# Attention and expert layer, one Trainium2 core: the context of four heads is split on GpSimd and turned by a DMA transpose

## The chip, the cores and the metric

The kernel runs on one core of one Trainium2 chip. The metric is the device time of one execution in microseconds (us), taken as the median of several runs.

## What is computed

The input x has 8 batches of 512 tokens with 256 features. The result is x plus two branches:

```python
xn = layernorm(x)
q, k, v = split(xn @ qkv_w.T)            # 16 heads of 64
q, k = rope(q), rope(k)
attn = softmax(q @ k.T / 8 - p * log1p(a * |i - j|))
out1 = concat_heads(attn @ v) @ out_w.T
out2 = top-1 mixture of 16 experts (relu(x @ w1) @ w2), capacity 256 rows each, scaled by the gate
result = x + out1 + out2
```

Everything is float32 in the reference. The kernel keeps that accuracy on TensorE by writing a float32 operand as the sum of two fp16 parts, a high and a low one, and by summing three products: high by high, high by low and low by high.

## The kernel before, in words

Three stages follow one another: `prepare` (norms, weights, routing), `experts`, and `attention`. The change lies wholly in `attention`, which fills the time from about 326 us to the end.

**Batches, groups and slots.** `attention` goes through 8 batches (the first and the last are written out, the six between are a hardware loop). A batch has 4 groups j of four heads, and a group has 8 slots k; slot l = 8j + k handles two tiles of 128 queries of one head. Each engine runs its own `slot(b, l)`, in an order that is written out by hand and held together by counting semaphores:

- TensorE: the scores of the slot (L1282, L1283), one "fill" of the PSUM bank `ps_x`, the transposes of the probabilities of slot l-1 into `ps_t` (L1294, 8 of them), and the products with the values of slot l-2 into `ps_o` (L1319, 24 of them).
- VectorE: the row minimum of the negated scores (L1187, twice), the reading of a fill, the low fp16 part of the turned probabilities (`pair_lo`, L1144), and after every fourth slot `read_context` (L1160, L1162), which divides `ps_o` by the sums of the softmax and writes the context `ctxt`.
- ScalarE: the copy of a fill, the high fp16 part of the turned probabilities (`pair_hi`, L1066), and two exponentials (L1085).

**Fills.** In slots k = 0 to 5 of a group TensorE projects the queries, keys and values of a group two ahead (`qk` L1249, `v` L1259). In slots k = 6 and 7 it multiplies the context of the group that ended one before by the output weights (`y`, L1269), and VectorE adds this to `yacc` (L1138).

**The context's way before the change.** The context of a group is complete when VectorE has done `read_context` in slot k = 2 of the next group. In slot k = 3 TensorE turns it (`context_transposes`, L1303, eight 128x128 transposes) into one of the two `ps_t` tiles that the probabilities use in turn. ScalarE writes its high part (`ctx_hi`, L1071) and VectorE its low part (`ctx_lo`, L1150) to `ot`, and the `y` fills of slots 6 and 7 read `ot`. The first group has no predecessor, and the last one's context is turned behind the last slot; so there are 32 such steps.

**GpSimd** rotates the queries and keys of the group two ahead: `turn` for w = 0 and 1 (four products L1003 into `prod`, a difference L1006 and a sum L1007 into `rot`), then the low parts (L1014) after ScalarE's high parts (L1060, in slots 5 and 7). In the groups j = 0 and 1 it also issues two gathers each (L1023).

**SyncE's queue** (SP) runs `move` once for each group that is projected: when GpSimd has written the second low part it issues 16 DMAs of 64 KB (L963), waits until they have landed, and issues two DMAs of 256 KB (`kswap`, L967). It also loads the next batch's activations (`xcur`, L970, in group j = 1) and the routes of a batch (L975, L976, at its start). ScalarE's queue stores `yacc` in slot 9 and loads it in slot 11 (L1094, L1097), 512 KB each.

Of the kernel before, what the change touches and what calls it, by code (L numbers as in the profile page):

```python
# [830 lines left out]
def attention(nc, sem, x, out, xt_dram, xcur, x_loaded, expert_dram, source_dram, gate_dram, ident, wt, wot, cos, sin,  # L831
# [8 lines left out]
    with ExitStack() as ctx:  # L840
# [4 lines left out]
        prod = sb("prod", [P, 4, S])  # L845
# [12 lines left out]
        ctxt = sb("ctxt", [P, TPB, HG * D])  # L858
        ot = [sb(f"ot_{n}", [P, 2, S], F16) for n in ("hi", "lo")]
# [44 lines left out]
        def pair_item(l):  # L904

            return 9 * (l // 8) + l % 8 + (l % 8 > 3)

        def items(b, n):

            if isinstance(b, int) and b == 0:  # L910
                return n + 1 - (n >= 0) - (n >= 4)
            return 36 * b + n + 1 - 2
# [83 lines left out]
        def _(pool):  # L996
            def turn(F, w, n):
# [4 lines left out]
                for i, (half, table) in enumerate(((0, cos), (1, sin), (0, sin), (1, cos))):  # L1002
                    nc.gpsimd.tensor_tensor(prod[:, i, :], proj[:, w, half, :], table[:], ALU.mult).then_inc(turned_parts, 1)  # L1003
                pool.wait_ge(turned_parts, done + 4)
                wait(pool, parts_lo, 2 * F - 1 + w)
                nc.gpsimd.tensor_tensor(rot[:, w, 0, :], prod[:, 0, :], prod[:, 1, :], ALU.subtract).then_inc(turned_parts, 1)  # L1006
                nc.gpsimd.tensor_tensor(rot[:, w, 1, :], prod[:, 2, :], prod[:, 3, :], ALU.add).then_inc(turned_parts, 1)  # L1007

            def step(F, fills):
                turn(F, 0, fills + 2)  # L1010
                turn(F, 1, fills + 4)
                for w in range(2):
                    pool.wait_ge(parts_hi, 2 * F + w + 1)
# [370 lines left out]
```

## Time and profile before

| | |
|---|---|
| Runs | 1440.41, 1443.87, 1444.68 us (median 1443.87) |
| Profiled execution, first to last instruction | 1431.5 us |
| Median less that span | 12.4 us |
| Mean granted TensorE clock | 0.945 of full speed over the span, 0.97 to 1.00 in the batches from 396 us on |
| One batch of `attention` in the loop | about 134 us |
| Busy from 664 to 797 us (133 us) | TensorE 127.3, weight loads 94.2, VectorE 104.7, ScalarE 101.7, GpSimd 80.6 us |

For the profiled execution the page gives the span alone; its time with what lies around the span is not given apart from the three runs. Busy times of TensorE are modelled from pipelined matmuls, so a busy share near one does not mean that it runs at its peak. A timeline lists the instructions of one engine in order of time; an idle time before an instruction stands in square brackets with the engine that ended it. `PEld` is the load of a matmul's weights, `SPq` an issue on SyncE's queue.

### The profile page before, as it was taken

How to read it: one execution, taken by the hardware profiler on the slowest of the kernel's cores; microseconds unless marked ns; L12 is line 12 of the kernel's file. 1: busy time of each engine (PE TensorE's matmuls, PEld its weight loads, DVE VectorE, ACT ScalarE, POOL GpSimd, SP SyncE). 2: the span in 40 equal slices, each digit the busy share in tenths (PEclk: the TensorE clock that was granted, in tenths of full speed). 3: DMA queues.
4: the chain of work that ended last, by engine and by line, in shares of the span. 5: the costliest groups of instructions: out<-in, count | busy, mean ns of one | idle time of the engine just before them, and what ended most of it. 6: DMA issues, size and time to landing. Idle time of an engine off the chain costs nothing.

```text
span 1431.5 us, 38280 instructions
## 1 busy us (share of the span) xinstructions
PE 1271.8 (89%) x13668; PEld 967.7 (68%) x13668; DVE 1109.8 (78%) x2166; ACT 1036.1 (72%) x1859; POOL 696.1 (49%) x536
## 2 busy tenths in 40 slices
PE   5622999995799999989998998999999999999996
PEld 5621888882477677767776776777677767777764
DVE  6873999973588887868886887788787868888885
ACT  3773888852688788768777787778688767877874
POOL 3064000004556666646655656566466646655600
PEclk8565999999899999999999999999999999999999
DMA  8554666621222223222312321132223212211220
GB/s 270 202 177 134 207 234 220 220 103 32 65 82 55 53 78 93 61 48 69 82 46 48 97 54 47 46 103 64 55 63 93 60 48 75 76 46 46 82 53 16
DMA packets 103602, 132.50 MB, mean 93 GB/s; under 512 B 17138, under 2 KB 89855, under 8 KB 103408
## 3 DMA queue, kind: packets, MB, share of 16 engines
q1 hardware_dynamic: 91136, 109.72, 26.4%
q0 software_dynamic: 4352, 12.41, 2.8%
q10 hardware_dynamic: 7920, 7.87, 1.7%
q8 instruction: 112, 1.84, 0.6%
q14 instruction: 82, 0.67, 0.2%
HBM read 58.79 MB, written 21.00 MB: 56 GB/s over the span
## 4 chain that ended last, share of the span: by engine, by line
PE 53%; ACT 7%; issue 7%; DVE 7%; SPq 1%; DVEq 1%; ACTq 0%; DMA 0%
PE ps_t L1294 13%; PE ps_x L1249 11%; PE ps_o L1319 8%; PE ps_s L1282 6%; PE ps_s L1283 6%; PE ps_x L1269 5%; ACT prob L1085 3%; DVE neg L1187 3%; PE ps_x L1259 3%; ACT ot_hi L1071 2%; DVE yacc L1172 1%; ACT pt_hi L1066 1%; SPq L963 1%; DVE yacc L1138 0%; DVE ctxt L1162 0%
## 5 line engine op out<-in xcount | busy, mean ns | idle before, releaser
L1144 DVE SCALAR_TENSOR_TENSOR pt_lo<-ps_t,pt_hi 128x1024 f16<-128x1024 f32 x256 | 312.6, 1221 | 155.2 <-ACT pt_hi L1066 155.2
L1187 DVE CUSTOM_DVE_ANT_0 neg<-ps_s,strips,score_scale 128x512 f32<-128x512 f32 x512 | 362.1, 743 | 31.9 <-PE ps_s L1283 28.1
L1085 ACT ACTIVATE prob<-neg,neg_max 128x512 f32<-128x512 f32 x512 | 362.9, 713 | 8.1 <-DVE neg_max L1187 8.1
L1066 ACT ACTIVATE pt_hi<-ps_t 128x1024 f16<-128x1024 f32 x256 | 262.0, 1023 | 113.4 <-PE ps_t L1294 113.0
L1014 POOL TENSOR_TENSOR parts<-rot,parts 128x1024 f16<-128x1024 f32 x62 | 132.2, 2134 | 307.5 <-ACT parts L1060 307.5
L1294 PE MATMUL ps_t<-ident,prob 128*128 128x128 f32 x2048 | 270.2, 274 | 3.8 <-ACT prob L1085 3.7
L1294 PEld LDWEIGHTS ps_t<-ident,prob 128*128 128x128 f32 x2048 | 236.5, 142 | 37.6 <-issue 9.3
L1282 PE MATMUL ps_s<-qk 128*128 128x512 f16 x512 | 198.1, 387 | 33.2 <-issue 18.4
L1319 PE MATMUL ps_o<-val_hi,pt_hi 128*128 128x64 f16 x2048 | 206.2, 193 | 14.5 <-DVE ctxt L1162 12.7
L1319 PE MATMUL ps_o<-val_hi,pt_lo 128*128 128x64 f16 x2048 | 206.2, 193 | 0.0
L1319 PE MATMUL ps_o<-val_lo,pt_hi 128*128 128x64 f16 x2048 | 206.2, 193 | 0.0
L1003 POOL TENSOR_TENSOR prod<-proj,cos 128x512 f32<-128x512 f32 x124 | 159.1, 1283 | 86.7 <-ACT proj L1051 84.0
L1283 PE MATMUL ps_s<-kswap,qk 128*128 128x512 f16 x512 | 197.3, 385 | 0.0
L1319 PEld LDWEIGHTS ps_o<-val_hi,pt_hi 128*128 128x128 f16 x2048 | 184.2, 98 | 18.8 <-issue 12.9
L1319 PEld LDWEIGHTS ps_o<-val_lo,pt_hi 128*128 128x128 f16 x2048 | 181.7, 98 | 2.7
L1319 PEld LDWEIGHTS ps_o<-val_hi,pt_lo 128*128 128x128 f16 x2048 | 181.9, 98 | 0.0
L1249 PE MATMUL ps_x<-xcur,wqkv_hi 128*128 128x512 f16 x512 | 158.0, 391 | 10.9 <-PEq L532 6.1
L1003 POOL TENSOR_TENSOR prod<-proj,sin 128x512 f32<-128x512 f32 x124 | 157.5, 1292 | 0.0
L1051 ACT COPY proj<-ps_x 128x512 f32<-128x512 f32 x124 | 72.6, 585 | 77.5 <-PE ps_x L1249 77.5
L1282 PEld LDWEIGHTS ps_s<-qk 128*128 128x128 f16 x512 | 50.2, 98 | 90.7 <-DVE neg_max L1187 42.1
L1249 PEld LDWEIGHTS ps_x<-xcur,wqkv_hi 128*128 128x128 f16 x512 | 50.8, 101 | 77.7 <-issue 13.8
L1249 PE MATMUL ps_x<-xcur,wqkv_lo 128*128 128x512 f16 x256 | 99.9, 390 | 0.0
(186 smaller groups left out, 2518.9 us busy)
## 6 DMA issues: line engine op xcount, KB each, us to landing
raw<-in_L_ffn_w_dram SPq DMA_DIRECT2D x32, 1024.0 KB, 6.7
qk<-parts SPq DMA_DIRECT2D x512, 64.0 KB
kswap<-qk SPq DMA_DIRECT2D x64, 256.0 KB
xa<-in_L_attn_x_dram SPq DMA_DIRECT2D x8, 512.0 KB, 6.9
xt_dram<-xth SPq DMA_DIRECT2D x8, 512.0 KB, 5.1
slots_dram<-zeros SPq DMA_DIRECT2D x4, 1024.0 KB, 8.4
xa<-slots_dram SPq DMA_DIRECT2D x16, 256.0 KB, 5.1
expert_dram<-xa POOLq DMA_DIRECT2D x16, 256.0 KB, 6.3
```

The lines of the kernel that those rows point to most:

```text
L1003: nc.gpsimd.tensor_tensor(prod[:, i, :], proj[:, w, half, :], table[:], ALU.mult).then_inc(turned_parts, 1)
L1014: nc.gpsimd.tensor_tensor(parts[:, 1, w], rot[:, w], parts[:, 0, w], ALU.subtract).then_inc(parts_lo, 1)
L1051: nc.scalar.copy(to[:, k // 2, k % 2, :], ps_x[:]).then_inc(x_free, 1)
L1066: nc.scalar.activation(pt[0][:, (l - 1) % 2].rearrange("p q k c -> p q (k c)"), ps_t[item % 2][:], ACT.Copy, scale=P_SCALE).then_inc(turne ...
L1085: nc.scalar.activation(prob[:, l % 2, q, :], neg[:, l % 2, q, :], ACT.Exp, bias=neg_max[:, 2 * (l % 2) + q:2 * (l % 2) + q + 1], scale=-1. ...
L1144: nc.vector.scalar_tensor_tensor(out=pt[1][:, (l - 1) % 2].rearrange("p q k c -> p q (k c)"), in0=ps_t[item % 2][:], scalar=P_SCALE, in1=p ...
L1187: nc.vector.tensor_tensor_reduce(neg[:, l % 2, q, :], ps_s[q][:], strips[:, h, start:start + S], score_scale[:, 0:1], 3.0e38, ALU.add, ALU ...
L1249: last = nc.tensor.matmul(ps_x[:], wt[a][:, kt, c:c + P], xcur[:, x, kt, :], start=(m == 0), stop=(m == 3 * KT - 1))
L1282: nc.tensor.matmul(ps_s[q][:], qk[:, j % 2, 0, k // 2, t:t + P], qk[:, j % 2, 1, k // 2, :], start=True, stop=False)
L1283: nc.tensor.matmul(ps_s[q][:], qk[:, j % 2, 0, k // 2, t:t + P], kswap[:, j % 2, k // 2, :], start=False, stop=True).then_inc(scored, 1)
L1294: last = nc.tensor.transpose(ps_t[item % 2][:, q, kt * P:(kt + 1) * P], prob[:, (l - 1) % 2, q, kt * P:(kt + 1) * P], ident[:])
L1319: last = nc.tensor.matmul(ps_o[:, c:c + D], pt[x][:, l % 2, q, kt, :], val[a][:, l2 // 8 % 4, kt, hd:hd + D], start=(m == 0), stop=(m == 3 ...
```

## The change

The eight TensorE transposes of the context, ScalarE's `ctx_hi` and VectorE's `ctx_lo` are taken out. VectorE's `read_context` writes half of a group's context (two heads, 128x512 float32) to a smaller `ctxt`; the factor that undoes `P_SCALE` moves into the reciprocal through one more small instruction. GpSimd splits each half into fp16 parts with a copy and a subtraction (`split_context`), the first half before the second low part of its step, the second half after the first four products of the next step. SyncE's queue then issues one DMA transpose of 128x2048 fp16 elements (512 KB) for each group, which writes `ot`. It stands ahead of the `move` of the same group and so behind the `move` of the group before. GpSimd's products are now written to `rot` and to a `prod` of half the size, and its difference and sum are done in place. The slots' `ps_t` tiles alternate without the context's turn between them.

```diff
-        prod = sb("prod", [P, 4, S])
+        prod = sb("prod", [P, 2, S])
...
-        ctxt = sb("ctxt", [P, TPB, HG * D])
-        ot = [sb(f"ot_{n}", [P, 2, S], F16) for n in ("hi", "lo")]
+        ctxt = sb("ctxt", [P, TPB, P])
+        ctx_parts = sb("ctx_parts", [P, 2, 2, TPB, P], F16)
+        ot = sb("ot", [P, 2, 2, S], F16)
...
+            def turn_context(b, j):
+
+                group = 4 * b + j
+                wait(sp, filled, y_fills(b, j))
+                sp.sem_inc(went_on)
+                sp.wait_ge(ctx_lo, 2 * group + 2)
+                sp.sem_inc(went_on)
+                sp.dma_start_transpose(ot[:].rearrange("p a k (t c) -> p (a k t) c", t=TPB),
+                                       ctx_parts[:].rearrange("p a k t c -> p (a k t c)")).then_inc(ctx_turned, 16)
...
             def batch(b):
                 load_routes(b)
                 for j in range(4):
+                    if j or not is_first(b):
+                        turn_context(b, j - 1)
                     if j == 1 and not is_last(b):
...
+            turn_context(NB - 1, 3)
...
+            def split_context(group, two):
+
+                unit = 2 * group + two
+                pool.wait_ge(ctx_read, unit + 1)
+                if not two:
+                    wait(pool, ctx_turned, 16 * group)
+                pool.sem_inc(went_on)
+                nc.gpsimd.tensor_copy(ctx_parts[:, 0, two], ctxt[:]).then_inc(ctx_hi, 1)
+                pool.wait_ge(ctx_hi, unit + 1)
+                nc.gpsimd.tensor_tensor(ctx_parts[:, 1, two], ctxt[:], ctx_parts[:, 0, two], ALU.subtract).then_inc(ctx_lo, 1)
+
+            def multiply(F, w, n):
 
                 done = 6 * (2 * F + w)
                 pool.wait_ge(x_free, n)
                 wait(pool, turned_parts, done)
-                for i, (half, table) in enumerate(((0, cos), (1, sin), (0, sin), (1, cos))):
-                    nc.gpsimd.tensor_tensor(prod[:, i, :], proj[:, w, half, :], table[:], ALU.mult).then_inc(turned_parts, 1)
+                wait(pool, parts_lo, 2 * F - 1 + w)
+                for half, tables in enumerate(((cos, sin), (sin, cos))):
+                    nc.gpsimd.tensor_tensor(rot[:, w, half, :], proj[:, w, 0, :], tables[0][:], ALU.mult).then_inc(turned_parts, 1)
+                    nc.gpsimd.tensor_tensor(prod[:, half, :], proj[:, w, 1, :], tables[1][:], ALU.mult).then_inc(turned_parts, 1)
+
+            def rotate(F, w):
+
+                done = 6 * (2 * F + w)
                 pool.wait_ge(turned_parts, done + 4)
-                wait(pool, parts_lo, 2 * F - 1 + w)
-                nc.gpsimd.tensor_tensor(rot[:, w, 0, :], prod[:, 0, :], prod[:, 1, :], ALU.subtract).then_inc(turned_parts, 1)
-                nc.gpsimd.tensor_tensor(rot[:, w, 1, :], prod[:, 2, :], prod[:, 3, :], ALU.add).then_inc(turned_parts, 1)
-
-            def step(F, fills):
-                turn(F, 0, fills + 2)
-                turn(F, 1, fills + 4)
-                for w in range(2):
-                    pool.wait_ge(parts_hi, 2 * F + w + 1)
-                    nc.gpsimd.tensor_tensor(parts[:, 1, w], rot[:, w], parts[:, 0, w], ALU.subtract).then_inc(parts_lo, 1)
+                nc.gpsimd.tensor_tensor(rot[:, w, 0, :], rot[:, w, 0, :], prod[:, 0, :], ALU.subtract).then_inc(turned_parts, 1)
+                nc.gpsimd.tensor_tensor(rot[:, w, 1, :], rot[:, w, 1, :], prod[:, 1, :], ALU.add).then_inc(turned_parts, 1)
+
+            def low(F, w):
+                pool.wait_ge(parts_hi, 2 * F + w + 1)
+                nc.gpsimd.tensor_tensor(parts[:, 1, w], rot[:, w], parts[:, 0, w], ALU.subtract).then_inc(parts_lo, 1)
+
+            def step(F, fills, ended=None, open_=None):
+                if F is not None:
+                    multiply(F, 0, fills + 2)
+                if ended is not None:
+                    split_context(ended, 1)
+                if F is not None:
+                    rotate(F, 0)
+                    multiply(F, 1, fills + 4)
+                    rotate(F, 1)
+                    low(F, 0)
+                if open_ is not None:
+                    split_context(open_, 0)
+                if F is not None:
+                    low(F, 1)
...
-                    if ahead(b, j):
-                        n, r, _ = ahead(b, j)
-                        step(2 * n + r, fills_before(b, 8 * j))
+                    n, r, _ = ahead(b, j) or (None, None, None)
+                    step(None if n is None else 2 * n + r, fills_before(b, 8 * j),
+                         None if is_first(b) and j == 0 else 4 * b + j - 1, 4 * b + j)
...
+            split_context(4 * NB - 1, 1)
...
-            def ctx_hi(b, item):
-                act.wait_ge(turned, items(b, item))
-                nc.scalar.activation(ot[0][:], ps_t[item % 2][:], ACT.Copy, scale=1.0 / P_SCALE).then_inc(turned_hi, 1)
...
-                if k == 3 and not (is_first(b) and j == 0):
-                    ctx_hi(b, 9 * j + 4)
...
-            def ctx_lo(b, item):
-                dve.wait_ge(turned_hi, items(b, item))
-                nc.vector.scalar_tensor_tensor(out=ot[1][:], in0=ps_t[item % 2][:], scalar=1.0 / P_SCALE, in1=ot[0][:],
...
-                if not two:
-                    wait(dve, turned, items(b, 9 * (l // 8) + 4))
-                nc.vector.reciprocal(rsum[:], sums[:, two, :]).then_inc(chain, 1)
-                dve.wait_ge(chain, unit + 1)
-                nc.vector.tensor_tensor(ctxt[:, :, two * P:two * P + P].rearrange("p t (h d) -> p h t d", h=2),
+                nc.vector.tensor_scalar(rsum[:], sums[:, two, :], P_SCALE, None, ALU.mult).then_inc(chain, 1)
+                dve.wait_ge(chain, 2 * unit + 1)
+                dve.sem_inc(went_on)
+                nc.vector.reciprocal(rsum[:], rsum[:]).then_inc(chain, 1)
+                dve.wait_ge(chain, 2 * unit + 2)
+                wait(dve, ctx_lo, unit)
+                dve.sem_inc(went_on)
+                nc.vector.tensor_tensor(ctxt[:].rearrange("p t (h d) -> p h t d", h=2),
...
+                                last = nc.tensor.matmul(ps_x[:, i * M:(i + 1) * M], ot[:, x, kt, t:t + P],
...
-            def context_transposes(b, item, units):
-                wait(pe, turned_lo, items(b, item - 2))
-                pe.wait_ge(ctx_read, units)
-                for kt in range(2):
-                    for t in range(TPB):
-                        last = nc.tensor.transpose(ps_t[item % 2][:, kt, t * P:(t + 1) * P],
-                                                   ctxt[:, t, kt * P:(kt + 1) * P], ident[:])
...
-                        pe.wait_ge(turned_lo, items(b, 9 * j + 4))
+                        pe.wait_ge(ctx_turned, 16 * (4 * b + j))
```

## Rows read from the trace of the kernel before

**Rows 1.** The page, part 4: the chain that ended last, by engine

```profile
PE 53%; ACT 7%; issue 7%; DVE 7%; SPq 1%; DVEq 1%; ACTq 0%; DMA 0%
```

**Rows 2.** Timeline of ScalarE, 700 to 720 us: start us, us, instruction, [idle before]

```profile
705.19 1.02 ACT L1066 ACTIVATE pt_hi<-ps_t 128x1024 f16<-128x1024 f32 x1 [0.28 <-PE ps_t L1294]
...
709.81 1.02 ACT L1066 ACTIVATE pt_hi<-ps_t 128x1024 f16<-128x1024 f32 x1 [0.29 <-PE ps_t L1294]
...
714.17 1.02 ACT L1066 ACTIVATE pt_hi<-ps_t 128x1024 f16<-128x1024 f32 x1 [0.29 <-PE ps_t L1294]
...
717.92 1.02 ACT L1066 ACTIVATE pt_hi<-ps_t 128x1024 f16<-128x1024 f32 x1 [0.39 <-PE ps_t L1294]
```

**Rows 3.** Timeline of TensorE's weight loads, slots k = 3 and 5

```profile
704.88 0.91 PEld L1303 LDWEIGHTS ps_t<-ident,ctxt 128*128 128x128 f32 x8
...
711.17 0.10 PEld L1282 LDWEIGHTS ps_s<-qk 128*128 128x128 f16 x1 [0.56 <-DVE neg_max L1187]
```

**Rows 4.** Timeline of VectorE, slots k = 2 to 4

```profile
699.92 0.19 DVE L1160 RECIPROCAL rsum<-sums 128x8 f32<-128x8 f32 x1
...
708.56 1.23 DVE L1150 SCALAR_TENSOR_TENSOR ot_lo<-ps_t,ot_hi 128x1024 f16<-128x1024 f32 x1 [1.09 <-ACT ot_hi L1071]
```

**Rows 5.** The page, part 5: groups, xcount | busy us, mean ns | idle before

```profile
L1014 POOL TENSOR_TENSOR parts<-rot,parts 128x1024 f16<-128x1024 f32 x62 | 132.2, 2134 | 307.5 <-ACT parts L1060 307.5
...
L1003 POOL TENSOR_TENSOR prod<-proj,cos 128x512 f32<-128x512 f32 x124 | 159.1, 1283 | 86.7 <-ACT proj L1051 84.0
```

**Rows 6.** Timeline of SyncE's queue, four groups of one batch's length

```profile
708.09 1.16 SPq L967 DMA_DIRECT2D kswap<-qk  x2
727.34 11.56 SPq L963 DMA_DIRECT2D qk<-parts  x16
740.37 1.15 SPq L967 DMA_DIRECT2D kswap<-qk  x2
...
772.22 1.89 SPq L967 DMA_DIRECT2D kswap<-qk  x2
...
812.95 1.16 SPq L967 DMA_DIRECT2D kswap<-qk  x2
814.98 0.61 SPq L970 DMA_DIRECT2D xcur<-xt_dram  x1
```

**Rows 7.** Timeline of TensorE: first matmul of slot k = 6's fill, same four groups

```profile
715.54 0.27 PE L1269 MATMUL ps_x<-wout_hi,ot_hi 128*128 128x256 f16 x1
...
748.68 0.27 PE L1269 MATMUL ps_x<-wout_hi,ot_hi 128*128 128x256 f16 x1
...
785.51 0.27 PE L1269 MATMUL ps_x<-wout_hi,ot_hi 128*128 128x256 f16 x1
...
817.00 0.27 PE L1269 MATMUL ps_x<-wout_hi,ot_hi 128*128 128x256 f16 x1
```

**Rows 8.** Timelines of SyncE's queue and TensorE: two groups that differ (loop's first, last batch)

```profile
511.40 0.80 SPq L976 DMA_DIRECT2D gate_now<-gate_dram  x1
...
516.23 0.27 PE L1269 MATMUL ps_x<-wout_hi,ot_hi 128*128 128x256 f16 x1
...
1372.95 1.15 SPq L967 DMA_DIRECT2D kswap<-qk  x2
...
1376.17 0.27 PE L1269 MATMUL ps_x<-wout_hi,ot_hi 128*128 128x256 f16 x1
```

**Rows 9.** DMA view, 812 to 820 us: GB/s in 40 slices of 0.2 us; issues, us to landing

```profile
GB/s 21 0 0 0 0 0 0 0 0 82 164 184 246 225 123 225 82 307 369 348 246 144 184 82 225 287 307 307 348 410 123 102 102 41 61 0 0 0 0 0
...
xcur<-xt_dram SPq DMA_DIRECT2D x1, 512.0 KB, 4.5
```

**Rows 10.** The page, part 3: a DMA queue's packets, MB, share of 16 engines' span

```profile
q10 hardware_dynamic: 7920, 7.87, 1.7%
```

**Rows 11.** Timeline of the last group's end, VectorE and TensorE

```profile
1417.40 0.69 DVE L1162 TENSOR_TENSOR ctxt<-ps_o,rsum 128x512 f32<-128x512 f32 x1
...
1422.38 0.39 PE L1269 MATMUL ps_x<-wout_hi,ot_hi 128*128 128x256 f16 x1 [2.38 <-DVE ot_lo L1150]
```

More of the change, by code:

```diff
@@ L882, in attention @@
         ctx_read = sem("ctx_read")
+        ctx_hi, ctx_lo, ctx_turned = sem("ctx_hi"), sem("ctx_lo"), sem("ctx_turned")
         filled, x_free = sem("filled"), sem("x_free")
@@ L902, in fills_before, with pairs_turned, y_fills @@
             return n
[L904 to L912, printed above, removed]
+        def pairs_turned(b, l):
+            return PAIRS * b + l
+        def y_fills(b, j):
+            return fills_before(b, 8 * j + 8)
         def wait(eng, s, v):
@@ L1083, in slot @@
                     if q == 0:
-                        wait(act, turned, items(b, pair_item(l - 1)))
+                        wait(act, turned, pairs_turned(b, l - 1))
                     nc.scalar.activation(prob[:, l % 2, q, :], neg[:, l % 2, q, :], ACT.Exp,
@@ L1119, in _ @@
             pair_hi(NB - 1, PAIRS)
-            ctx_hi(NB - 1, 37)
         @block.vector
@@ L1141, in pair_lo @@
             def pair_lo(b, l):
-                item = pair_item(l)
-                dve.wait_ge(turned_hi, items(b, item))
-                nc.vector.scalar_tensor_tensor(out=pt[1][:, (l - 1) % 2].rearrange("p q k c -> p q (k c)"), in0=ps_t[item % 2][:],
+                dve.wait_ge(turned_hi, pairs_turned(b, l))
+                nc.vector.scalar_tensor_tensor(out=pt[1][:, (l - 1) % 2].rearrange("p q k c -> p q (k c)"), in0=ps_t[l % 2][:],
                                                scalar=P_SCALE, in1=pt[0][:, (l - 1) % 2].rearrange("p q k c -> p q (k c)"),
-                                               op0=ALU.mult, op1=ALU.subtract).then_inc(turned_lo, 1)
-            def ctx_lo(b, item):
-                dve.wait_ge(turned_hi, items(b, item))
-                nc.vector.scalar_tensor_tensor(out=ot[1][:], in0=ps_t[item % 2][:], scalar=1.0 / P_SCALE, in1=ot[0][:],
                                                op0=ALU.mult, op1=ALU.subtract).then_inc(turned_lo, 1)
@@ L1194, in slot @@
                     pair_lo(b, l)
-                if k == 3 and not (is_first(b) and j == 0):
-                    ctx_lo(b, 9 * j + 4)
                 if l == 13:
@@ L1268, in fill @@
                             for x, a in PARTS:
-                                last = nc.tensor.matmul(ps_x[:, i * M:(i + 1) * M], ot[x][:, kt, t:t + P],
+                                last = nc.tensor.matmul(ps_x[:, i * M:(i + 1) * M], ot[:, x, kt, t:t + P],
                                                         wot[a][:, 2 * g + kt, :], start=(m == 0), stop=(m == 5))
@@ L1288, in transposes @@
                 s = PAIRS * b + l
-                item = pair_item(l)
-                wait(pe, turned_lo, items(b, item - 2))
+                wait(pe, turned_lo, pairs_turned(b, l - 2))
                 for q in range(2):
@@ L1293, in transposes @@
                     for kt in range(TPB):
-                        last = nc.tensor.transpose(ps_t[item % 2][:, q, kt * P:(kt + 1) * P],
+                        last = nc.tensor.transpose(ps_t[l % 2][:, q, kt * P:(kt + 1) * P],
                                                    prob[:, (l - 1) % 2, q, kt * P:(kt + 1) * P], ident[:])
-                last.then_inc(turned, 1)
-            def context_transposes(b, item, units):
-                wait(pe, turned_lo, items(b, item - 2))
-                pe.wait_ge(ctx_read, units)
-                for kt in range(2):
-                    for t in range(TPB):
-                        last = nc.tensor.transpose(ps_t[item % 2][:, kt, t * P:(t + 1) * P],
-                                                   ctxt[:, t, kt * P:(kt + 1) * P], ident[:])
                 last.then_inc(turned, 1)
@@ L1335, in slot @@
                     transposes(b, l)
-                if k == 3 and not (is_first(b) and j == 0):
-                    context_transposes(b, 9 * j + 4, PAIRS // 4 * b + 2 * j)
                 if l >= 2 or not is_first(b):
@@ L1352, in _ @@
             values(NB - 1, PAIRS + 1)
-            context_transposes(NB - 1, 37, PAIRS // 4 * NB)
-            pe.wait_ge(turned_lo, items(NB - 1, 37))
+            pe.wait_ge(ctx_turned, 16 * 4 * NB)
             for k in range(2):
```

9 lines of the change are left out of this document (3 added, 6 removed).

## The prediction, made before the changed kernel ran

> **What bounds the kernel now.** I read the chain of waits first: more than half of the span lies on TensorE, and ScalarE, VectorE and issue have 7% each [rows 1]. So most of what is taken from TensorE inside `attention` should come off the time, if nothing is late in its place. Then the timeline of ScalarE, whose `pt_hi` starts once in each slot and is a clock for slots. From slot 5 to 6 it takes 717.92 - 714.17 = 3.75 us. From slot 3 to 4 it takes 4.62 us, and from 4 to 5 it takes 4.36 us [rows 2]. These are the two slots that the context's turn touches. The eight transposes hold the weight loads for 0.91 us in slot 3. In slot 5 the scores then wait 0.56 us for VectorE [rows 3], which has been kept 1.09 us waiting for `ot_hi` and 1.23 us by `ot_lo` at 708.56 [rows 4]. Last I read SyncE's queue beside the first `y` matmul of slot 6, since the new transfer has to fit between the two [rows 6, 7].
>
> **What goes.** Slot 3 gives back 4.62 - 3.75 = 0.87 us and slot 4 gives 4.36 - 3.75 = 0.61 us, so 1.48 us for each group that has a predecessor. There are 31 of these: 45.9 us. ScalarE's 1.0 us and VectorE's 1.23 us are in this already, as they lay beside TensorE's work except for the 0.61 us.
>
> **What comes, VectorE.** One more small instruction for each `read_context`, like the reciprocal's 0.19 us [rows 4], 64 in all. In slot 2 VectorE has idle time for it; in slot 6 it can push the next minimum back. Against it stands a small refund: a TensorE that waits in slot 6 lets VectorE catch up. I set the two against each other and count nothing; if the cover is gone they cost 32 x 0.2 = 6 us.
>
> **What comes, GpSimd.** The copy and the subtraction of 128x512 are not in the trace. The low part of 128x1024 to fp16 takes 2134 ns, so half is 1.07 us; a float32 product of 128x512 takes 1283 ns [rows 5]. A pair costs 2.1 to 2.6 us, 4.9 us for a group. GpSimd waits 307.5 us before its low parts [rows 5], 5 us each, and the first half's split goes there. The second half's split stands behind four products. Even if these began only when `read_context` ends at about 700.9, the split would end at 700.9 + 4 x 1.28 + 2.6 = 708.6 us, and SyncE's queue is busy until 708.09 + 1.16 = 709.25 us [rows 4, 5, 6]. So the queue, not GpSimd, is what the transfer waits for. The in-place difference and sum cost what they did.
>
> **What comes, SyncE's queue.** This is the price that decides. `turn_context` stands behind the `move` of the group before, thus behind the end of `kswap`'s issue, and `y` in slot 6 waits for the landing. Call T the time from the end of `kswap`'s issue to the landing. The room for it is
>
> - group j = 1: 817.00 - 814.11 = 2.9 us
> - group j = 2: 715.54 - 709.25 = 6.3 us
> - group j = 3: 748.68 - 741.52 = 7.2 us
> - group j = 0: 785.51 - 774.11 = 11.4 us, of which the two issues of the routes take 1.5
>
> [rows 6, 7]. Two groups differ: the first j = 0 of the loop has 516.23 - 512.20 = 4.0 us, and j = 2 of the last batch, whose slots have no projections, has 1376.17 - 1374.10 = 2.1 us [rows 8]. From all of these 1.48 us go, since slot 6 comes earlier by what slots 3 and 4 give. What is left: 1.4 (8 groups), 4.8 (7), 5.7 (7), 8.4 (6), 2.5 (1) and 0.6 us (1). A stall does not wear off: the next `move` begins after ScalarE's work of slot 7, so the queue is late by as much as TensorE, and each group pays T less its room anew. Behind the issue itself nothing waits: the next is `xcur` or a `move` that comes later.
>
> **T itself** is not in the trace. The nearest row is the load of `xcur`: also 512 KB, also right behind `kswap`. It is issued at 814.98 and lands 4.5 us later, that is 5.4 us after `kswap`'s issue ended. The slices show why: `kswap`'s 512 KB move until about 816.2 us, and the next 512 KB until about 818.8 us [rows 9]. Issued at once and moved as fast, the transpose would land near T = 4.5 us; that is the lower bound. For the upper one I let it go in pieces of one row of a 128x128 block, 256 bytes: 2048 pieces, 128 for each of 16 engines. A packet of 1 KB on ScalarE's queue takes 0.017 x 1431.5 x 16 / 7920 = 49 ns [rows 10], so the pieces would take 6.3 us in place of 2.6 us, and T = 9.1 us. I take T = 6.5 us: above the plain copy, since small pieces and the generation of many descriptors are not free, and nearer to it than to the packet bound, as that packet is four times as long.
>
> The Trainium skill, page "Advanced Engine Details and Errata", section "X-Bar Transpose (TRN2)", says that transposing DMAs on this chip are as fast as regular ones. By that T would be 5.4 us and the sum 1443 us; no row here shows it.
>
> **The sum** at T = 6.5 us: 8 x 5.1 + 7 x 1.7 + 5.9 + 7 x 0.8 + 4.0 = 68.2 us of new stalls, less 45.9 us. At the very end there is no cover. Today 1422.38 - 1418.09 = 4.3 us pass from the context to the first `y` matmul [rows 11]. Afterwards it is the split, 2.5 us, and T without `kswap` ahead, 6.5 - 2.1 = 4.4 us, so 2.6 us more. Together +25 us: the profiled span of 1431.5 would become 1456, and with the 12.4 us that lie around it, which stay, the median of 1443.9 becomes 1469 us.
>
> **The rivals.**
>
> 1. The transfer is quick, T = 4.5 us. Stalls 8 x 3.1 + 3.9 + 2.0 = 30.7 us, end 0.6 us: 30.7 - 45.9 + 0.6 = -14.6, so 1429 us, faster. This is the other side, and it decides below T of about 5.4 us. For it: the DMA engines are idle before 813.8 and after 818.8 [rows 9], and only j = 1 has little room. Against it: it takes all of a plain copy's speed and no descriptor time. With T near 4 it would reach 1424 us.
> 2. It lands as `xcur` does, T = 5.4 us: stalls 43.9, end 1.5, so -0.5 and 1443 us, no change.
> 3. The blocks are handed out one after another by the queue. A plain issue takes 11.56 / 16 = 0.72 us [rows 6]; sixteen blocks of 128x128 would take 11.6 us, and T = 13.5 us with the last one's landing. Stalls 266.8, end 11.7: 1676 us. For it: nothing in the trace shows how a transpose is issued. Against it: it is one instruction. The Trainium skill, page "VectorE: DVE Perf Modes", section "The three transpose paths", gives 1309 ns for a 128x128 block of 16-bit elements by DMA. If sixteen went in series, an estimate from that figure is T = 21 us and about 1904 us.
> 4. The transfer is hidden, but it slows `kswap` or the small moves, so `qk` comes late. Scores need it a group later, with room of tens of microseconds, so I give it no chance of its own.
>
> **How the numbers follow.** Forecast, T from 5.7 to 9.1 us: 0.52, with 1469 us at its likeliest point and 1538 us at its end (stalls 134.8, end 5.2). Rival 1: 0.28. Rival 2: 0.10. Rival 3 and anything above 9.1 us: 0.10. A difference of 0.3%, 4.3 us, is about what a measurement of this kernel tells from no change. That makes faster 0.28, same 0.10, slower 0.62. The range goes from 1424 us (rival 1's end) to 1540 us and leaves out rival 3 and a little below. As both signs have much of the chance: the forecast's own range is 1450 to 1538 us.
>
> **What would show it.** TensorE's first `y` load of slot 6 idle in nearly each group, most in j = 1 (near 5 us) and little or nothing in j = 0; its releaser the DMA that writes `ot`; the issue of the transpose right behind `kswap`'s; `pt_hi` at 3.75 us from slot 3 to 4 and from 4 to 5; GpSimd's splits done before that issue. The forecast is wrong if `ot` lands less than 5 us after `kswap`'s issue, if the wait before it is GpSimd's, or if slots 3 and 4 keep their length.

## The result and the profile after the change

The changed kernel takes 1527.4 us (median; 1520.6 to 1535.4), beside 1443.7 us before: a ratio of 1.061, 95% interval 1.057 to 1.066. It is slower, as forecast, but by 84 us and not by 25, and mostly by another mechanism than the one forecast. Its profiled span is 1522.7 us.

The page of the changed kernel, part 4, the chain that ended last by engine and by line, is to be compared with [rows 1]:

```profile
PE 45%; DVE 11%; issue 9%; ACT 5%; SPq 3%; DMA 3%; POOL 1%; DVEq 1%; POOLq 0%; ACTq 0%
PE ps_t L1321 10%; PE ps_x L1277 10%; PE ps_o L1337 8%; PE ps_s L1310 5%; PE ps_s L1311 5%; PE ps_x L1287 4%; DVE rsum L1186 4%; ACT pt_hi L1107 4%; PE ps_x L1297 3%; SPq L963 3%; DVE ctxt L1193 2%; DVE yacc L1203 1%; DVE neg L1218 1%; DVE yacc L1172 1%; DMA ot<-ctx_parts 1%
```

TensorE fell from 53% to 45% and VectorE rose from 7% to 11%. `DVE rsum L1186` alone has 4% of 1522.7, some 60 us. That is the small instruction that multiplies 8 sums in each partition by `P_SCALE`. The tile view of `rsum` (count, then duration in ns, min/median/max) shows how an instruction of that size gets there:

```profile
L1186 DVE TENSOR_SCALAR rsum<-sums x64: 157/165/3524, 390.4 to 1505.2; 128x8 f32<-128x8 f32 x64
L1189 DVE RECIPROCAL rsum<-rsum x64: 202/203/205, 390.7 to 1505.5; 128x8 f32<-128x8 f32 x64
```

The reciprocal of the same 8 elements behind it never took more than 205 ns. The timeline of VectorE has the slots 2 and 6 of a group j = 2, then a slot 2 of a group j = 3 and one of a group j = 0:

```profile
725.74 3.44 DVE L1186 TENSOR_SCALAR rsum<-sums 128x8 f32<-128x8 f32 x1
729.33 0.20 DVE L1189 RECIPROCAL rsum<-rsum 128x8 f32<-128x8 f32 x1
729.71 0.69 DVE L1193 TENSOR_TENSOR ctxt<-ps_o,rsum 128x512 f32<-128x512 f32 x1 [0.18 <-DVE rsum L1189]
...
744.30 0.16 DVE L1186 TENSOR_SCALAR rsum<-sums 128x8 f32<-128x8 f32 x1
...
761.67 1.23 DVE L1186 TENSOR_SCALAR rsum<-sums 128x8 f32<-128x8 f32 x1
...
513.57 0.33 DVE L1186 TENSOR_SCALAR rsum<-sums 128x8 f32<-128x8 f32 x1
```

GpSimd's timeline over the first of these stretches, and the two products around 513.57:

```profile
724.21 1.28 POOL L1028 TENSOR_TENSOR rot<-proj,cos 128x512 f32<-128x512 f32 x1
725.43 1.28 POOL L1029 TENSOR_TENSOR prod<-proj,sin 128x512 f32<-128x512 f32 x1
726.66 1.27 POOL L1028 TENSOR_TENSOR rot<-proj,sin 128x512 f32<-128x512 f32 x1
727.89 1.25 POOL L1029 TENSOR_TENSOR prod<-proj,cos 128x512 f32<-128x512 f32 x1
730.57 0.61 POOL L1017 CAST ctx_parts<-ctxt 128x512 f16<-128x512 f32 x1 [1.42 <-DVE ctxt L1193]
731.26 1.16 POOL L1019 TENSOR_TENSOR ctx_parts<-ctxt,ctx_parts 128x512 f16<-128x512 f32 x1
...
512.61 1.27 POOL L1029 TENSOR_TENSOR prod<-proj,sin 128x512 f32<-128x512 f32 x1
513.83 1.28 POOL L1028 TENSOR_TENSOR rot<-proj,sin 128x512 f32<-128x512 f32 x1
```

The last of the four products ends at 729.14 us and the tensor_scalar at 729.18. It began 0.3 us into the second of them and ended with the fourth. Of the 32 slots 2, 15 look like this, with 3.4 to 3.5 us; 6 (of groups j = 3) have 1.2 us, where it began in the fourth product; 6 (of groups j = 0) have 0.33 us, and 5 have 0.16 us. Those of 0.33 us began near the end of the second product and were through at the change to the third, with no gap between the two. So the wait is not always for the end of all products, and what decides between these cases the traces do not show. In slot 6, where GpSimd waits, it takes 0.16 us. TensorE pays for the long ones in slot 2 (its timeline):

```profile
730.46 0.20 PE L1337 MATMUL ps_o<-val_hi,pt_hi 128*128 128x64 f16 x1 [3.22 <-DVE ctxt L1193]
```

The clock for slots, `pt_hi` on ScalarE, shows what this costs. From slot 2 to 3 the kernel before takes 705.19 [rows 2] - 701.46 = 3.73 us in a group j = 2:

```profile
701.46 1.02 ACT L1066 ACTIVATE pt_hi<-ps_t 128x1024 f16<-128x1024 f32 x1 [0.20 <-PE ps_t L1294]
```

The changed kernel takes 7.34 us in the group j = 2 shown above and 9.96 us in a group j = 1:

```profile
727.27 1.02 ACT L1107 ACTIVATE pt_hi<-ps_t 128x1024 f16<-128x1024 f32 x1 [0.19 <-PE ps_t L1321]
...
734.61 1.02 ACT L1107 ACTIVATE pt_hi<-ps_t 128x1024 f16<-128x1024 f32 x1 [0.29 <-PE ps_t L1321]
...
979.16 1.02 ACT L1107 ACTIVATE pt_hi<-ps_t 128x1024 f16<-128x1024 f32 x1 [0.20 <-PE ps_t L1321]
...
989.12 1.02 ACT L1107 ACTIVATE pt_hi<-ps_t 128x1024 f16<-128x1024 f32 x1 [0.44 <-PE ps_t L1321]
```

The tensor_scalar takes 3.44 us in both, and TensorE waits 3.2 us for `ctxt` in both. What differs is TensorE's granted clock behind the wait, the third number from the end in the view by stretches (us; busy us of PE, PEld, DVE, ACT and POOL; granted clock, DMA share, GB/s):

```profile
731.00:733.00 2.00, 1.97 (x20) 0.87 (x17) 2.00 (x6) 1.52 (x4) 1.92 (x3) 1.00 0.42 102
...
983.00:985.00 2.00, 2.00 (x19) 1.18 (x17) 1.82 (x4) 1.50 (x4) 1.92 (x3) 0.50 0.41 98
985.00:987.00 2.00, 2.00 (x7) 0.63 (x5) 1.44 (x4) 0.00 (x0) 1.75 (x2) 0.50 0.18 41
```

At 0.50, the lower of its two levels (1.2 in place of 2.4 GHz), a matmul of the projection takes 0.63 us and not 0.38. Of the 15 slots 2 with the long tensor_scalar, 13 took 8.8 to 10.0 us and two took 7.3. Added over all groups, the stretch from slot 2 to 3 is 110 us longer than before. An estimate of the clock's share, from the slots of 8.4 to 10.0 us against those of 7.3 (j = 1 and 2) and 7.0 us (j = 3), is 41 us.

The transfer on which the forecast was built looks different. The timeline of SyncE's queue is to be compared with [rows 6], and the tile view of `ot` gives its landing:

```profile
733.48 2.11 SPq L967 DMA_DIRECT2D kswap<-qk  x2
735.95 2.21 SPq L976 DMA_TRANSPOSE ot<-ctx_parts  x1
...
768.14 1.16 SPq L967 DMA_DIRECT2D kswap<-qk  x2
769.67 3.54 SPq L976 DMA_TRANSPOSE ot<-ctx_parts  x1
```

```profile
DMA to landing us min/median/max: 3.6/5.8/10.6
```

And in the waits of the changed kernel between 530 and 1400 us (in total us, times, longest us) TensorE's waits for `ot` are small beside those for `ctxt`:

```profile
PEld ps_o L1337 <- DVE ctxt L1193: 69.4, 46, 3.5
PE ps_o L1337 <- DVE ctxt L1193: 59.5, 23, 3.2
...
PE ps_x L1297 <- DMA ot<-ctx_parts: 2.1, 2, 1.2
PEld ps_x L1297 <- DMA ot<-ctx_parts: 1.4, 1, 1.4
```

That window leaves out the two ends. Over all groups the stretch from slot 5 to 6, in which the first `y` fill waits, is 11 us longer than before, and 7 of these are in one group, j = 2 of the last batch.

Slots 3 and 4 became short, as forecast. The `pt_hi` clock is to be compared with [rows 2]: 3.75 us from slot 3 to 4 and 3.75 us from slot 4 to 5. From slot 2 to 3 this group j = 3 takes 7.00 us, where the kernel before has 5.40 in the groups j = 3:

```profile
761.32 1.02 ACT L1107 ACTIVATE pt_hi<-ps_t 128x1024 f16<-128x1024 f32 x1 [0.20 <-PE ps_t L1321]
...
768.32 1.02 ACT L1107 ACTIVATE pt_hi<-ps_t 128x1024 f16<-128x1024 f32 x1 [0.29 <-PE ps_t L1321]
...
772.07 1.02 ACT L1107 ACTIVATE pt_hi<-ps_t 128x1024 f16<-128x1024 f32 x1 [0.29 <-PE ps_t L1321]
...
775.82 1.02 ACT L1107 ACTIVATE pt_hi<-ps_t 128x1024 f16<-128x1024 f32 x1 [0.29 <-PE ps_t L1321]
```

### The profile page after: what moved, and what is told of

It reads as the page before. It is cut to its first block, busy times and chain, and to the rows that moved or that the text cites. A ratio compares the mean times of both kernels' runs of the same rounds, so it can differ in the third digit from the quotient of the medians.

```text
span 1522.7 us, 37788 instructions
## 1 busy us (share of the span) xinstructions
PE 1292.1 (85%) x13412; PEld 961.2 (63%) x13412; DVE 1143.6 (75%) x2198; ACT 1008.9 (66%) x1827; POOL 804.9 (53%) x664
## 4 chain that ended last, share of the span: by engine, by line
PE 45%; DVE 11%; issue 9%; ACT 5%; SPq 3%; DMA 3%; POOL 1%; DVEq 1%; POOLq 0%; ACTq 0%
PE ps_t L1321 10%; PE ps_x L1277 10%; PE ps_o L1337 8%; PE ps_s L1310 5%; PE ps_s L1311 5%; PE ps_x L1287 4%; DVE rsum L1186 4%; ACT pt_hi L1107 4%; PE ps_x L1297 3%; SPq L963 3%; DVE ctxt L1193 2%; DVE yacc L1203 1%; DVE neg L1218 1%; DVE yacc L1172 1%; DMA ot<-ctx_parts 1%
## 5 line engine op out<-in xcount | busy, mean ns | idle before, releaser
L1337 PE MATMUL ps_o<-val_hi,pt_hi 128*128 128x64 f16 x2048 | 214.8, 196 | 77.3 <-DVE ctxt L1193 75.0
L1321 PEld LDWEIGHTS ps_t<-ident,prob 128*128 128x128 f32 x2048 | 241.4, 144 | 43.9 <-issue 18.1
L1310 PE MATMUL ps_s<-qk 128*128 128x512 f16 x512 | 207.0, 404 | 24.9 <-issue 17.0
L1337 PE MATMUL ps_o<-val_hi,pt_lo 128*128 128x64 f16 x2048 | 214.8, 196 | 0.0
L1337 PE MATMUL ps_o<-val_lo,pt_hi 128*128 128x64 f16 x2048 | 214.6, 196 | 0.0
L1311 PE MATMUL ps_s<-kswap,qk 128*128 128x512 f16 x512 | 207.0, 404 | 0.0
L1277 PE MATMUL ps_x<-xcur,wqkv_hi 128*128 128x512 f16 x512 | 173.3, 424 | 10.9 <-PEq L532 6.1
L1028 POOL TENSOR_TENSOR rot<-proj,cos 128x512 f32<-128x512 f32 x62 | 78.9, 1272 | 114.6 <-ACT proj L1093 92.2
L1297 PE MATMUL ps_x<-wout_hi,ot 128*128 128x256 f16 x512 | 98.4, 280 | 18.9 <-DMA ot<-ctx_parts 16.5
L1277 PE MATMUL ps_x<-xcur,wqkv_lo 128*128 128x512 f16 x256 | 107.0, 418 | 0.0
L632 POOL DMA_DIRECT2D expert_dram<-xa x16 | 11.5, 720 | 180.1 <-ACT xa L673 180.1
```

Source lines behind the costliest of these rows:

```text
L1028: nc.gpsimd.tensor_tensor(rot[:, w, half, :], proj[:, w, 0, :], tables[0][:], ALU.mult).then_inc(turned_parts, 1)
L1277: last = nc.tensor.matmul(ps_x[:], wt[a][:, kt, c:c + P], xcur[:, x, kt, :], start=(m == 0), stop=(m == 3 * KT - 1))
L1297: last = nc.tensor.matmul(ps_x[:, i * M:(i + 1) * M], ot[:, x, kt, t:t + P], wot[a][:, 2 * g + kt, :], start=(m == 0), stop=(m == 5))
L1310: nc.tensor.matmul(ps_s[q][:], qk[:, j % 2, 0, k // 2, t:t + P], qk[:, j % 2, 1, k // 2, :], start=True, stop=False)
L1311: nc.tensor.matmul(ps_s[q][:], qk[:, j % 2, 0, k // 2, t:t + P], kswap[:, j % 2, k // 2, :], start=False, stop=True).then_inc(scored, 1)
L1321: last = nc.tensor.transpose(ps_t[l % 2][:, q, kt * P:(kt + 1) * P], prob[:, (l - 1) % 2, q, kt * P:(kt + 1) * P], ident[:])
```

## The experiments

Theory A: the tensor_scalar has to wait for GpSimd's products. Rival B: the transfer and GpSimd's splits cost the time. Theory C came up on the way: whatever lengthens the chain of instructions ahead of `ctxt` costs its full length. All ratios are to the kernel before, run on the same chip in the same series.

### The tensor_scalar alone, in the kernel before (before_plus_scale)

```diff
-                nc.vector.reciprocal(rsum[:], sums[:, two, :]).then_inc(chain, 1)
+                nc.vector.tensor_scalar(rsum[:], sums[:, two, :], 1.0, None, ALU.mult).then_inc(chain, 1)
+                dve.wait_ge(chain, 2 * unit + 1)
...
+                nc.vector.reciprocal(rsum[:], rsum[:]).then_inc(chain, 1)
+                dve.wait_ge(chain, 2 * unit + 2)
```

> The kernel before with one addition: a tensor_scalar of 128x8 (times 1.0) ahead of the reciprocal in read_context, and its semaphore wait. Nothing goes to GpSimd or to a DMA transpose. Theory A (the small tensor_scalar is what costs: in slot 2 of a group it can't run while GpSimd is in its products, and holds VectorE for 1.2 to 3.5 us in place of 0.16): 1495 to 1535 us, the tensor_scalar's mean near 1.1 us with two kinds, slot 6 at 0.16 us and slot 2 at 1 to 3.5 us. Rival B (the DMA transpose and the splits on GpSimd make the changed kernel slow): 64 x 0.2 us at most, 1444 to 1457 us, and no tensor_scalar above 0.3 us.

Measured 1545.5 us, ratio 1.074 (1.067 to 1.080). This addition of one small instruction for each `read_context`, with neither GpSimd's splits nor a DMA transpose, costs 105 us, more than the whole change. That is above the expected 1495 to 1535 us. Its tile view:

```profile
L1160 DVE TENSOR_SCALAR rsum<-sums x64: 159/164/3514, 389.0 to 1525.3; 128x8 f32<-128x8 f32 x64
```

So rival B isn't needed for the changed kernel's 84 us. What its transfer costs there, scale_folded and after_turn_early show below.

### The same instruction in an odd shape (before_scale_odd)

```diff
-        sums = sb("sums", [P, 2, 8])
+        sums = sb("sums", [P, 2, 9])
+        wide = sb("wide", [P, 3, 4])
...
+                nc.vector.tensor_scalar(wide[:, :, 0:3], sums[:, two, :].rearrange("p (a c) -> p a c", a=3), 1.0, None, ALU.mult).then_inc(chain, 1)
...
+                nc.vector.reciprocal(rsum[:].rearrange("p (a c) -> p a c", a=3), wide[:, :, 0:3]).then_inc(chain, 1)
```

> before_plus_scale with the tensor_scalar on 9 elements, read as one row of 9 and written as 3 rows of 3 at a pitch of 4, so that the outermost counts are odd and differ; one of the 9 is a constant. The Trainium skill, page Vector Engine (DVE) Microarchitecture Reference, section on the perf modes, gives such a shape no two-port mode, and page SBUF - State Buffer ties the lock against GpSimd to that mode. Theory A1 (the two-port mode is what waits): tensor_scalar 0.2 us in every slot, 1441 to 1460 us. Theory A2 (a tensor_scalar waits for GpSimd in any shape): as before_plus_scale, 1530 to 1560 us.

Measured 1467.9 us, ratio 1.020 (1.015 to 1.025), 77 us less than with 8 elements in one row. Its tile view:

```profile
L1161 DVE TENSOR_SCALAR wide<-sums x64: 148/151/161, 398.2 to 1446.2; 128x9 f32<-128x9 f32 x64
```

All 64 take at most 161 ns, beside the same products of GpSimd: in 29 of the 32 slots 2 they began 0.2 to 1.2 us into one of them. It is not the operation and not its place that waits, but the form. A1 holds for the duration. The time was 8 us above the expected range, though: the link itself costs 29 us, which led to theory C.

### Two more reciprocals in the kernel before (before_three_reciprocals)

```diff
                 nc.vector.reciprocal(rsum[:], sums[:, two, :]).then_inc(chain, 1)
+                dve.wait_ge(chain, 3 * unit + 1)
...
+                nc.vector.reciprocal(rsum[:], rsum[:]).then_inc(chain, 1)
+                dve.wait_ge(chain, 3 * unit + 2)
...
+                nc.vector.reciprocal(rsum[:], rsum[:]).then_inc(chain, 1)
```

> The kernel before with two more reciprocals of 128x8 in read_context, each with its wait: a longer chain than that of before_plus_scale, 2 x (0.20 + 0.18) = 0.76 us for each of 64, but of an operation that was never slow beside GpSimd. Theory A (it is the tensor_scalar's form that waits for GpSimd): 1441 to 1465 us, no reciprocal above 0.25 us. Rival C (anything that lengthens the chain ahead of ctxt costs 100 us): 1500 us and more.

Measured 1502.1 us, ratio 1.042 (1.033 to 1.051): 63 us more, beyond the range for theory A and in that of the recorded rival C. VectorE's timeline shows each link and its gap:

```profile
770.82 0.19 DVE L1160 RECIPROCAL rsum<-sums 128x8 f32<-128x8 f32 x1
771.15 0.20 DVE L1163 RECIPROCAL rsum<-rsum 128x8 f32<-128x8 f32 x1
771.75 0.20 DVE L1166 RECIPROCAL rsum<-rsum 128x8 f32<-128x8 f32 x1 [0.40 <-DVE rsum L1163]
772.10 0.69 DVE L1169 TENSOR_TENSOR ctxt<-ps_o,rsum 128x512 f32<-128x512 f32 x1
```

From the first reciprocal to `ctxt` 1.28 us pass here and 1.04 us at the next unit (792.18 to 793.22), where the kernel before has 0.23 (699.92 [rows 4] to 700.15). That is 0.81 to 1.05 us more, and 64 times as much is 52 to 67 us, around the 63 us measured. The `pt_hi` clock divides them otherwise: 0.7 to 0.8 us more from slot 2 to 3 in the groups j = 0, 1 and 2, and 0.8 to 1.2 us more from slot 6 to 7. In the groups j = 3 it is 0.8 us more from slot 2 to 3 in two of them and 2.0 to 3.4 us in the other six. In one of the six, from 751.87 us, the granted clock was 0.66 from 755 to 760 us. So most of the longer chain is on TensorE's path in both slots, and some of the 63 us is the clock. No reciprocal took more than 205 ns, so the wait of theory A and the length of the chain are two costs of different kinds.

### The scale without an instruction of its own (scale_folded)

```diff
-                nc.vector.tensor_scalar(rsum[:], sums[:, two, :], P_SCALE, None, ALU.mult).then_inc(chain, 1)
...
-                nc.vector.tensor_tensor(ctxt[:].rearrange("p t (h d) -> p h t d", h=2),
+                for h in range(2):
+                    last = nc.vector.scalar_tensor_tensor(
+                        out=ctxt[:, :, h * D:h * D + D], in0=ps_o[:].rearrange("p (h t d) -> p h t d", h=2, t=TPB)[:, h],
+                        scalar=1.0 / P_SCALE, in1=rsum[:, h * TPB:h * TPB + TPB].unsqueeze(2).to_broadcast([P, TPB, D]),
+                        op0=ALU.mult, op1=ALU.mult)
```

> The changed kernel without the tensor_scalar: the factor 1/P_SCALE goes into the instruction that reads ps_o, which becomes two scalar_tensor_tensor of 128x256 with ps_o in PSUM as their first input. Theory A: the waits of TensorE for ctxt in slot 2 go, and what is left is the sum of the prediction with the transfer's measured time (T near 5.9 us): +10 us on 1443.7, so 1435 to 1465 us, with TensorE now waiting for the transposed context in group j = 1. Rival B: 1515 to 1530 us, as little has changed.

Measured 1454.7 us, ratio 1.011 (1.007 to 1.014); in a second series 1452.3 us, 1.009 (1.005 to 1.013). 73 us of the changed kernel's 84 go with that instruction. What shows now is the forecast's own mechanism. Waits of scale_folded from 530 to 1400 us:

```profile
PE ps_x L1296 <- DMA ot<-ctx_parts: 34.8, 16, 4.8
PEld ps_x L1296 <- issue: 28.5, 12, 3.7
```

Its timelines of SyncE's queue and TensorE's weight loads, and the DMA view of 700 to 740 us, give T, the time from the end of `kswap`'s issue to the landing, in a group j = 2:

```profile
721.25 1.16 SPq L967 DMA_DIRECT2D kswap<-qk  x2
722.77 2.96 SPq L976 DMA_TRANSPOSE ot<-ctx_parts  x1
...
727.90 0.10 PEld L1296 LDWEIGHTS ps_x<-wout_hi,ot 128*128 128x128 f16 x1 [1.16 <-issue]
...
ot<-ctx_parts SPq DMA_TRANSPOSE x1, 5.0
```

`kswap`'s issue ends at 722.41, the transpose is issued at 722.77 and lands 5.0 us later: T = 5.4 us, and the `y` weights load 0.1 us after that. This is the landing of the plain `xcur` load [rows 9] to the tenth. Over the 30 groups with a `kswap` ahead, T is 4.4 to 7.9 us, with a median of 5.4. In the changed kernel it is 4.4 to 11.0 us, with a median of 6.3.

The `pt_hi` clock gives the account of this run's slots against those of the kernel before: the stretches from slot 3 to 5 are 45.8 us shorter in all, the one from slot 5 to 6 is 59 us longer, that from slot 2 to 3 is 4 us longer, and those from slot 6 to 7 and from 7 on are 8 us shorter.

### The changed kernel with the odd shape (after_scale_odd)

The edit is that of before_scale_odd with `P_SCALE` as the factor.

> The changed kernel with its tensor_scalar in the odd shape of before_scale_odd, nothing else. If the wait for GpSimd is what separates the changed kernel from scale_folded, the tensor_scalar takes 0.15 us in each of 64 and the time is scale_folded's plus 64 links of 0.33 us: 1465 to 1485 us. If the wait is a symptom of something else in the changed kernel: 1510 us and more.

scale_folded ran again beside it:

> scale_folded as before, for comparison on the same chip: 1445 to 1460 us.

Measured 1473.5 us, ratio 1.023 (1.016 to 1.030), beside scale_folded's second series of 1452.3 us. The wait for GpSimd is then worth 0.061 - 0.023 = 0.038 of 1440 us, 56 us, and the link 21 us. The 64 tensor_scalars of the changed kernel were busy 67 us in all, where 64 x 0.15 are 10 us. That this difference of 57 us is so near to 56 is chance. By the `pt_hi` clock the changed kernel's stretches from slot 2 to 3 are 98 us longer than here, 41 of them with the clock by the estimate above, and its stretches from slot 5 to 6 are 50 us shorter: the wait in slot 2 hides most of the lateness of the transfer. In the kernel before, where it hides nothing, the same change of shape was worth 77 us.

### What the transfer costs (folded_no_turn, folded_turn_early)

folded_no_turn leaves the DMA transpose out of scale_folded, so the context isn't turned, and lets the `y` fills wait for GpSimd's split alone:

```diff
-                                last = nc.tensor.matmul(ps_x[:, i * M:(i + 1) * M], ot[:, x, kt, t:t + P],
+                                last = nc.tensor.matmul(ps_x[:, i * M:(i + 1) * M], ctx_parts[(l // 8 - 1) % 2][:, x, kt, t // P, :],
...
-                        pe.wait_ge(ctx_turned, 16 * (4 * b + j))
+                        pe.wait_ge(ctx_lo, 2 * (4 * b + j))
```

> scale_folded with the DMA transpose left out: the y fills read the split context as it stands, unturned, from two buffers in turn, so the output is not the layer's. It prices the transfer alone: with theory A 1395 to 1412 us, that is 1443.7 less the 45.9 us that slots 3 and 4 give back, and scale_folded less this is what the transfer's lateness costs (near 50 us by the prediction's stalls). If the transfer is hidden, both are equal.

folded_turn_early keeps it and moves its issue into the move before it:

```diff
                         sp.dma_start(qk[32 * q:32 * q + 32, r, :, h, :], parts[rows, q // 2, :, q % 2, :]).then_inc(qk_moved[r], 16)
+                if turn:
+                    turn_context(*turn)
                 sp.wait_ge(qk_moved[r], MOVED * n + 256)
```

> scale_folded with the DMA transpose issued inside the move before it, between the 16 DMAs of 64 KB and the wait for their landing, so ahead of kswap. If T behind kswap is what is left (theory A with the stalls of the prediction), the transpose lands 3 to 6 us earlier and the stalls in slot 6 go: 1400 to 1430 us. If the transpose was hidden anyway, it equals scale_folded within 0.5%.

folded_no_turn: 1402.7 us, ratio 0.972 (0.966 to 0.978). folded_turn_early: 1403.6 us, 0.974 (0.967 to 0.980), and 1398.3 us, 0.971 (0.968 to 0.975), in a second series, just below what was expected there. So the transfer's lateness cost scale_folded 52 us (1454.7 - 1402.7), and issuing it ahead of `kswap` gives all of it back. The tile view of `ot` in folded_turn_early:

```profile
DMA to landing us min/median/max: 3.6/4.1/6.7
```

### The early issue in the changed kernel (after_turn_early)

The changed kernel with folded_turn_early's move, its tensor_scalar left in.

> The changed kernel, tensor_scalar included, with only the DMA transpose moved ahead of kswap, as in folded_turn_early. If the tensor_scalar alone makes the changed kernel slow and the transpose is covered by the time lost in slot 2: 1500 to 1527 us, at most 20 us less than the changed kernel. If the two costs add: 1460 to 1480 us, 50 us less, as between scale_folded and folded_turn_early.

Measured 1517.4 us, ratio 1.055 (1.049 to 1.061), in the expected 1500 to 1527 us. The same edit that gives 51 us without the tensor_scalar gives about 10 us with it, and as the two intervals overlap, these 10 are not certain. TensorE's stall in slot 2 falls while the queue still issues the 16 DMAs ahead of `kswap` (973.56 to 984.47 us around the tensor_scalar of 977.62 to 981.06). Slot 6 comes later by it and `kswap` doesn't, so the transfer lands within time that is lost already: there at 993.63 us, 4.1 us ahead of its `y` fill. The two costs don't add. Taking out the instruction gives 73 us, taking out the lateness about 10, and taking out both gives 124 (1527.4 - 1403.6).

### The reciprocal one slot earlier (before_recip_ahead, folded_early_recip_ahead)

```diff
+            def invert_sums(l):
+                nc.vector.reciprocal(rsum[:], sums[:, (l - 6) // 4 % 2, :]).then_inc(chain, 1)
...
-                nc.vector.reciprocal(rsum[:], sums[:, two, :]).then_inc(chain, 1)
...
+                if l % 4 == 1 and not (is_first(b) and l == 1):
+                    invert_sums(l + 1)
```

> The kernel before with one edit: the reciprocal of the sums is issued one slot earlier, behind the two minima of slot l % 4 = 1, so that only the multiplication stands between the last product with the values and TensorE's next use of ps_o. Theory C (this chain is on TensorE's path in slots 2 and 6, each of its links costing what it takes): 64 x 0.23 to 0.35 us less than the kernel before, 1418 to 1430 us. If slot 2 has idle time for such an instruction, as the prediction said, at most slot 6's half: 1432 to 1441 us.

> folded_turn_early with the reciprocal one slot earlier in the same way. Theory C: 15 to 22 us below folded_turn_early, 1380 to 1392 us. Otherwise 1396 to 1405 us.

folded_turn_early ran again beside them:

> folded_turn_early as before, for comparison on the same chip: 1399 to 1410 us.

Measured 1430.7 us, ratio 0.995 (0.992 to 0.998), and 1392.1 us, 0.968 (0.965 to 0.972), beside folded_turn_early's second series of 1398.3 us. Both miss the 15 to 22 us of theory C: 6 us in either kernel. A link more costs most of its length, a link less gives about a quarter of it. The `pt_hi` clock of before_recip_ahead says why. From slot 2 to 3 the kernel before had 3.73 us already, about the length of a slot that nothing holds up, and nothing could be won; from slot 6 to 7 it had 3.82 us and now has 3.75. The chain stood just at the edge of TensorE's path, not deep in it. folded_early_recip_ahead is the fastest version here, 3.2% below the kernel before. Its interval overlaps that of folded_turn_early (0.968 to 0.975), so the last 6 us are likely and not certain.

## Why the prediction was wrong

**What bounds the kernel, what goes.** Right in kind and in size. Slots 3 and 4 are 3.75 us each, against the 4.62 and 4.36 us of [rows 2], and over all groups they are 45.7 us shorter, against the forecast's 45.9. folded_no_turn, where nothing is late, is 38 us faster in all, with the longer chain of two `ctxt` instructions in it.

**What comes, VectorE: the step that failed.** I priced the tensor_scalar "like the reciprocal's 0.19 us", wrote that "in slot 2 VectorE has idle time for it", and counted nothing, or 6 us at most. The runs show 73 us for it in the changed kernel (scale_folded) and 105 us in the kernel before (before_plus_scale). Three things make this up.

- The instruction waits for GpSimd's products. It took 3.44 us at 725.74 and 1046 ns on the mean, where the odd shape took 0.15. The wait was worth 56 us in the changed kernel and 77 us in the kernel before.
- The link itself, in any form, lies between the last product with the values and `ctxt`, where TensorE waits for `ps_o`: 21 us. The time that VectorE has to spare lies elsewhere, before `pt_lo` (1.16 us idle before the one at 724.60, just ahead of the row at 725.74).
- Behind TensorE's long wait in slot 2 its granted clock fell to 0.50 for some microseconds in most groups. This is an estimated 41 us of the changed kernel's longer slots, and it is contained in the figures above.

I priced an instruction by another one of its size, not of its form. The Trainium skill, page "SBUF — State Buffer", section "Who interferes with whom", states that a tensor_scalar in a two-port mode and a GpSimd instruction lock each other out for a whole instruction, and that one with a single SBUF input outside these modes doesn't. By that rule an estimate of the wait is up to 1.3 us, one product. The trace agrees with a wait for GpSimd, and differs in how long: in 15 of 32 slots 2 it lasted over three products in a row, 3.4 us. That the odd shape took 151 ns fits the rule on the modes; the mode itself is in no trace.

**What comes, GpSimd.** Right: the copy takes 0.61 us and the subtraction 1.16 us, 1.8 us in place of 2.1 to 2.6, and the queue was not waiting for them (the split ends at 732.42 us and `kswap`'s issue at 735.59).

**What comes, SyncE's queue; T.** The mechanism was right. T was taken as 6.5 us. It is 6.3 us in the median of the changed kernel and 5.4 us in that of scale_folded, the value of rival 2 and of a plain copy. The pieces were as small as the upper bound had them: by part 3 of the two pages 32 transposes added 66560 packets and 16.78 MB, about 2080 packets of 252 bytes each. But by the shares there a packet took about 28 ns, an estimate, and not 49. In scale_folded, where T is the plain copy's, the rule cited from the Trainium skill, page "Advanced Engine Details and Errata", section "X-Bar Transpose (TRN2)", is borne out.

The stalls of scale_folded stood where they were forecast, but the sum for T = 5.4 us was too low: 43.9 us were forecast and the stretches from slot 5 to 6 are 59 us longer. The groups j = 1 have 4.4 us each, where 4.0 were forecast, and the groups j = 2 of the first seven batches have 12 us together in place of 4.2; 5 of these 12 are in the first batch, where T was 7.8 us. In all, the slots of its profiled execution are 10 us longer than those before and the end is 1.6 us longer (1.5 were forecast). The first products with the values stand 6 us later, at 382.3 us against 376.1, and that lies ahead of the changed part.

In the changed kernel itself the mechanism hardly shows: 11 us from slot 5 to 6 in place of 68, though T was nearly as forecast. The stall of the tensor_scalar came first and covered it. The forecast of the sign was right by luck, for another reason than the one given.

**The rivals.** None had VectorE wait for GpSimd. Rival 3, sixteen blocks in series, is out: the issue takes 1.6 to 5.1 us and not 11.6. What would have shown the forecast wrong was named ("the forecast is wrong if `ot` lands less than 5 us after `kswap`'s issue, if the wait before it is GpSimd's ..."), and not what happened: another wait ahead of it.

**TensorE's clock.** The prediction has no term for it. The granted clock over the span is 0.906 in the changed kernel, 0.945 before and 0.946 in scale_folded, where TensorE's long stalls for `ctxt` are gone. In scale_folded it also falls to 0.50 behind the stalls of the groups j = 1 (696 to 698 us), so part of its 59 us may be the clock as well. No run changes the clock by itself.

## What to carry to other kernels

Price an added VectorE instruction by its form and by what GpSimd does at that moment, and look for the same form in the trace: a reciprocal, a tensor_scalar and an instruction that reads PSUM are three different things beside a busy GpSimd. Ask also where in the slot an idle engine is idle, since time ahead of a wait does not pay for an instruction behind it. When TensorE stands still for some microseconds, look at its granted clock behind the stall: here a stall of 3.2 us for a tensor_scalar of 3.44 us cost 3.6 us of time in two groups and 5.1 to 6.3 us in 13. Don't add the costs of two stalls that can cover each other; take each out alone and both together. A transfer that is late may be cured by its place in the queue. Here it was late by 4.4 us in one group of four and by less in the others; its place was worth 51 us and turned a change that lost into one that gains 3%.

## What the runs showed of the hardware that I had not expected

- A tensor_scalar of 128x8 float32 from SBUF to SBUF took 3.44 us when it began 0.3 us into the second of four GpSimd products of 1.27 us each, and 0.16 us beside an idle GpSimd. It did not get in at the two changes from one product to the next. In 6 cases that began 0.97 us into a product it got in at the next change, in 0.33 us, so back-to-back products do not always keep it out. Read as a row of 9 and written as 3 rows of 3 it took 148 to 161 ns in all 64 cases.
- After TensorE had waited 3.2 us at a granted clock of 1.00, the clock was 0.50 from 983 to 987 us, and 1.00 again from 989 us. After the same wait at 727 us it stayed at 1.00.
- A DMA transpose of 128x2048 fp16 elements, SBUF to SBUF, lands as soon as a plain 512 KB load issued in the same place (T = 5.4 us both, in the median of scale_folded), though it takes the queue 1.6 to 5.1 us to issue in the changed kernel where a plain one takes 0.4 to 0.6.
